# A run's last two head sums placed in front of the next run's bonus sums on TensorE

## The reference

```python
xm = xa[:, :, None] + sx[:, :, None] * (maa_stack + xxx)
xk, xw, xv, xr, xg = (xm[:, :, j] for j in range(5))
w = jnp.exp(-jnp.exp(time_decay + jnp.tanh(xw @ td_w1) @ td_w2))
r = xr @ Wr.T; k = xk @ Wk.T; v = xv @ Wv.T; g = jax.nn.silu(xg @ Wg.T)
def step(s, rkvw):
    r_t, k_t, v_t, w_t = rkvw
    a = k_t[..., :, None] * v_t[..., None, :]
    out = jnp.einsum('bhi,bhij->bhj', r_t, u * a + s)
    s = a + w_t[..., :, None] * s
    return (s, out)
```

## Time and profile before

| what | value |
|---|---|
| median of 3 runs | 1139.03 us (1138.09 to 1141.67) |
| the profiled execution | 1138.86 us, its span 1137.1 us |
| mean granted TensorE clock | 0.988 of full speed |
| busy PE, DVE, ACT, POOL | 1070.2, 910.3, 704.3, 591.4 us |
| the merged loop, bodies 0 to 15 | about 510 to 1070 us of the span |
| one body in the middle of it | 34.78 us |

### The profile page before, as it was taken

The page is one execution under the profiler, slowest core; times in us unless marked ns, Lnnn a source line. Parts: engine busy times, 40 slices in busy tenths (PEclk is TensorE's granted clock), DMA queues, the critical chain, the costliest instruction groups (busy, mean ns, idle before and its releaser), DMA issues.

```text
span 1137.1 us, 34405 instructions
## 1 busy us (share of the span) xinstructions
PE 1070.2 (94%) x12992; PEld 897.9 (79%) x12992; DVE 910.3 (80%) x1677; ACT 704.3 (62%) x1606; POOL 591.4 (52%) x520
## 2 busy tenths in 40 slices
PE   5899999999999999899999999999999998887798
PEld 4789888888889887788777778777787776666677
DVE  5987777888777784238998898988989999899964
ACT  4778787778777775455544555545565445545574
POOL 4778877877878873034444344343444443343121
PEclk9999999999999998999999999999999999889999
DMA  9400000011111110033213333123331133304011
GB/s 330 163 4 1 0 0 3 5 48 40 40 47 37 43 32 2 1 85 79 57 42 75 84 85 76 31 60 83 83 83 47 45 75 84 77 7 121 19 37 56
DMA packets 39867, 65.01 MB, mean 57 GB/s; under 512 B 4384, under 2 KB 26208, under 8 KB 39392
## 3 DMA queue, kind: packets, MB, share of 16 engines
q1 hardware_dynamic: 39776, 63.75, 21.1%
HBM read 55.35 MB, written 8.39 MB: 56 GB/s over the span
## 4 chain that ended last, share of the span: by engine, by line
PE 81%; DVE 10%; issue 5%; ACT 3%; POOL 1%; DMA 0%; DVEq 0%; ACTq 0%; POOLq 0%
PE psum L982 10%; PE psum L991 10%; PE psum L353 9%; PE psum L1071 6%; PE psum L267 5%; PE psum L336 5%; PE psum L368 5%; PE psum L297 3%; PE psum L280 3%; PE psum L1031 3%; PE psum L1109 2%; PE psum L1142 2%; PE psum L1251 2%; DVE shared L1763 2%; PE psum L310 2%
## 5 line engine op out<-in xcount | busy, mean ns | idle before, releaser
L1763 DVE TENSOR_TENSOR_SCAN shared<-late_wT,shared 128x512 f32<-128x512 f32 x128 | 169.9, 1328 | 0.0
L892 POOL TENSOR_TENSOR late_xm<-late_mixed,late_xa 128x512 f32<-128x512 f32 x64 | 91.3, 1436 | 111.4 <-DVE late_mixed L1729 111.1
L232 POOL TENSOR_TENSOR shared<-shared,att_row_max 128x512 f32<-128x512 f32 x128 | 132.6, 1056 | 17.8 <-DVE att_row_max L564 17.8
L353 PE MATMUL psum<-shared 128*128 128x128 f32 x1024 | 127.3, 278 | 1.0 <-ACT shared L462 1.0
L453 ACT ACTIVATE shared<-shared 128x512 f32<-128x512 f32 x128 | 80.5, 631 | 69.8 <-POOL shared L232 69.6
L353 PEld LDWEIGHTS psum<-shared 128*128 128x128 f32 x1024 | 121.4, 195 | 1.4 <-ACT shared L462 1.4
L982 PE MATMUL psum<-late_glnT,w 128*128 128x256 f32 x512 | 119.8, 387 | 1.8 <-ACT late_glnT L1359 1.8
L991 PE MATMUL psum<-w,late_hT 128*128 128x256 f32 x512 | 118.6, 380 | 1.0 <-ACT late_hT L1368 0.9
L564 DVE TENSOR_REDUCE att_row_max<-shared 128x8 f32<-128x512 f32 x128 | 86.8, 680 | 40.5 <-POOL shared L225 40.5
L901 POOL TENSOR_TENSOR shared<-shared,late_rT 128x512 f32<-128x512 f32 x32 | 40.7, 1273 | 142.7 <-DVE shared L1763 142.7
L982 PEld LDWEIGHTS psum<-late_glnT,w 128*128 128x128 f32 x512 | 95.9, 192 | 18.1 <-issue 2.8
(11 more groups left out here) (167 smaller groups left out, 2436.6 us busy)
## 6 DMA issues: line engine op xcount, KB each, us to landing
shared<-v_rows SPq DMA_DIRECT2D x64, 512.0 KB, 7.4
shared<-in_enc SPq DMA_DIRECT2D x64, 128.0 KB, 2.6
v_rows<-shared SPq DMA_DIRECT2D x64, 64.0 KB, 1.8
out<-x SPq DMA_DIRECT2D x16, 256.0 KB, 2.0
x<-in_x SPq DMA_DIRECT2D x7, 512.0 KB, 10.1
w<-in_w SPq DMA_DIRECT2D x2, 1024.0 KB, 16.9
shared<-in_cross_mask SPq DMA_DIRECT2D x1, 1024.0 KB, 11.6
shared<-in_w_qkv SPq DMA_DIRECT2D x1, 768.0 KB, 4.6
```

Source lines behind the costliest of these rows:

```text
L232: nc.gpsimd.tensor_tensor(zs, zs, peak.unsqueeze(2).to_broadcast([P, PAIRS, S]), ALU.subtract).then_inc(shifted, 1)
L353: last = nc.tensor.matmul(dst[:, half * P:(half + 1) * P], w[:, kb, c0 + half * P:c0 + (half + 1) * P], src[:, u % 2, kb, 0:P], start=(kb ...
L892: nc.gpsimd.tensor_tensor(xm[m % XM].rearrange("p h (b t) -> p (h b) t", t=S), mixed[:, m % 2, :, :].rearrange("p h (b t) -> p (h b) t", t=S),
L1763: nc.vector.tensor_tensor_scan(states, wT[:, u, half, :, :, :].rearrange("p j b t -> p (j b t)"), states, 0.0, ALU.mult, ALU.add).then_inc ...
```

## The change

In PE's body the two calls of `sum_heads` for run s-1 stand ahead of `bonus_sums(s)` instead of behind it. Nothing else is different, on any engine: the same instructions, the same waits, the same buffers.

```diff
                 if early(s):
                     ch_transpose(early_run(s, 0), 0)
-                if now:
-                    bonus_sums(s)
                 if old:
                     sum_heads(s - 1, 2)
                     sum_heads(s - 1, 3)
+                if now:
+                    bonus_sums(s)
                 if there(s - 2):
                     project_out(s - 2)
```

## The result

The changed kernel takes 1127.48 us in the median of 7 executions (1123.08 to 1130.46), the kernel before beside it 1139.31 (7 executions, 1136.76 to 1142.15). The ratio is 0.9894, with a 95% interval of 0.9874 to 0.9914: faster by 1.1%. The prediction was 1128.0, with a range of 1124.5 to 1132.5. The profiled execution took 1127.48 us with a span of 1125.7, 11.38 us less than the one of before.

What follows compares the result with a forecast made beforehand. PE was taken to bound the middle of the loop, VectorE bodies 13 to 15. Eleven bodies at 1.00 us give 11.0: 1138.86 - 11.0 = 1127.9, with 0.17 for the median 1128.0 us; range 1124.5 to 1132.5.

Steps and rivals of the forecast that it cites:

- The bound and the place: Bodies 2 to 12: PE bounds, its one listed wait the bonus sums for VectorE's gate, 11 times, 9.0 us.
- the 11.0 of the sum: Whole kernel: 11 bodies gain 1.00 us each, 11.0 us; body 1 and bodies 13 to 15 gain nothing.
- The hole from start to start: PE between WgT and the bonus sums: 0.97 us a body counted by group starts, against 0.81 idle in the row.
- the restart's 0.08: Bonus sums on PE: 1.04 us after the wait against 0.96 without, so 0.08 may go with the wait.
- Narrow and wide groups, net 0: PE's weight switches cost 0.08 into narrow and about 0.10 into wide; same two before and after, net 0.
- The margin of 0.11 at the bonus sums: Bonus sums could start at 713.43 and are allowed to at 713.32, so no wait for the gate is left.
- rival A: A new wait, as at the bonus sums, takes part: gain 0.3 to 0.8 a body, 1130.2 to 1135.6 us; chance 0.08.
- The margin at L1031: `mix_pair` in the middle bodies: residual L1826 reaches PE about 721.15, L1031 wants to start at 721.36; free by 0.2.
- VectorE catches up: VectorE gains 0.84 at L1729 and makes up the other 0.16 at its waits for keys and at L1697.
- Rival B: VectorE becomes the bound, deciding under 32.2 us a body; if its gaps were rigid, 1139, no change; chance 0.04.
- The last bodies, nothing: Bodies 13 to 15: PE waits for VectorE anyway, no gain or loss; L1782 covered by 0.12 in body 15.
- Rival C: TensorE's clock in bodies 13 to 15: a half-speed stretch moves, 3.2 us either way, 1124.8 to 1131.2; chance 0.07.

Runs made afterwards that it cites:

- The kernel with exchanged banks: Against the kernel before, order kept: bonus sums and output projection exchange PSUM banks, so the bonus sums need no gate; 1127.76 us, ratio 0.9924.
- the kernel with fewer switches: Changed kernel with the mixer's matmuls, narrow group first, directly behind the head sums, ahead of bonus sums and output projection; 1129.1 us, ratio 0.993.
- the two late gates: Changed kernel with VectorE's gate of run s-2 moved behind the second scan and read (1172.97 us), or only behind that scan (1145.5 us).
- the two half changes: Kernel before with the swap only in bodies 2 to 12 (1127.34 us, ratio 0.9914), or only in 1 and 13 to 15 (1138.62 us, 1.0006).
- the half cover: Kernel before with only one of the two head sums moved ahead of the bonus sums, the other left behind; 1135.9 us, ratio 0.9967.
- the kernel with the late gate: Changed kernel with VectorE's gate of run s-2 later by one key_values, one scan and one read; 1172.97 us, ratio 1.0302.

## Why the prediction was right

- *The bound and the place.* Right: PE bounds the bodies 2 to 12 and had one wait there. With the swap in these bodies alone they were as short as with the whole change, with it in the others alone nothing was gained.
- *The time.* 1128.0 against 1127.48 is closer than the parts deserve, and that is luck. The eleven bodies gave 0.57 more than the 11.0 of the sum, body 1 another 0.15 and the start of the loop 0.55, which the change can't explain; the last bodies took 0.89 back.
- *The size.* The hole from start to start, 0.97, with the restart's 0.08 makes 1.05, and 1.02 to 1.06 were measured. I had taken 1.00 of bounds of 0.82 and 1.07. The idle time in PE's row, 0.82, would have been a fifth too small. The kernel with exchanged banks shows both parts without a new order.
- *Narrow and wide groups, net 0.* Right: the old order without the wait has the same body. Their size is larger than the 0.18 that I had read for a pair. Into narrow weights it is 0.09 (1.82 against 1.73 for WgT), out of them 0.10 on the wide group (0.97 against the 0.87 that the bonus sums take behind a wide group in the kernel with fewer switches), and another 0.11 on the narrow group itself (the head sums take 1.00 in front of a wide group and 0.89 in front of a narrow one). That is 0.30, near the 0.32 of that kernel.
- *The margin of 0.11 at the bonus sums.* Measured 0.10; no wait in any body (rival A did not come about; its lower gain was 11 x 0.3 = 3.3 us and not 3.4). The margin at L1031, forecast at 0.2, was 0.13, and the kernel with fewer switches used it up. What a lost margin costs the two late gates show: 1.57 us for 1.53 us of wait.
- *VectorE catches up.* Right in the result, wrong in a number: its wait for the keys was to stay at 0.7 to 0.9 and fell to 0.34. The step was that VectorE's work from L1729 on keeps its length. The scan behind L1729 took 2.00 instead of 1.54 (at 726.43 in the trace of before), since it met GpSimd at another moment. 0.88 - 0.16 - 0.46 = 0.26 is near the 0.34. Rival B's point, 32.2 us for a body, is therefore too low: 33.73 - 0.34 - 0.78 = 32.6.
- *The last bodies, nothing.* Wrong by 0.9 of the 11.6 us. L1782 did not wait for the bonus sums, as predicted. But of the 0.71 that body 13 lost, 0.50 lies between WgT and the second part of the mixer: L1031 starts 955.81 - 941.42 = 14.39 behind WgT, where it was 13.89, and waits 4.96 us for the residual L1826 instead of 4.46. On VectorE the step is one scan, which meets GpSimd's L875 0.22 us after that began, and not 0.73 after, and takes 1.89 instead of 1.38. The sum took every duration on VectorE as fixed. That this comes from the middle bodies, and not from the swap in body 13, the two half changes show. The remaining 0.21, and the 0.18 of body 14, come behind L1031; the stretch at the half clock lies over other groups there, but that it is their cause is not shown.
- *Rival C, the clock.* In the two profiled executions it changed nothing: 0.988 of full speed in both, and 0.93 over the 46.30 us in both. The seven executions of the changed kernel have mean clocks of 0.983 to 0.992 and times of 1130.46 to 1123.08, in that order; the one in the middle had 0.988 and 1127.48. From kernel to kernel the executions spread over 1.6 to 7.4 us, and that is the noise of the comparisons here. So differences of a few us, such as 3.8 by the ratio against 4.6 by the bodies for the half cover, are told apart by the length of the bodies alone.

## What to carry to other kernels

Where the bounding engine waits for another, look in its own order for work that needs no such wait, and count the hole from start to start, not by the idle time in the row: that gives how much cover is wanted and what it brings. Look at the wait's cause too, since a shared buffer can be the whole of it, and exchanging two banks here did the same as the new order. Check how late the delayed instruction becomes for its own readers, above all in the stages that another engine bounds, and don't take that engine's durations as fixed when the work beside it moves.

## What the runs showed of the hardware

**A wait of 2.27 us, once in 37 us of otherwise full work, can take TensorE's clock to the half level.** In the kernel with the late gate eleven bodies had this wait in the same place. In the first of them the granted clock stayed at 1.00; in the ten that followed it fell to the half level and cost 1.56 us per body beyond the wait. In body 14 a wait of 2.14 at the bonus sums left the next groups at 1.00 again. A wait of 1.53 in the same place, and the 0.81 of the kernel before, left the clock at the full level in all eleven bodies. So the length of the wait does not decide alone, and what else does no run here shows. The Trainium skill, page "TensorE: Matmul & The Clock Gate", section "🎯 Why this matters for your kernels", advises against idle gaps of TensorE between bursts of matmuls, and the gap that it names is longer than 2.27 us. Here 2.27 was too much ten times out of eleven; the measurement decides.

**VectorE's scan and a GpSimd sum don't run beside each other.** Whichever began second took longer, by nearly all the time that the first still had to run: 2.00 and 2.09 against 1.22 for the scan in the middle bodies (0.92 and 1.01 us were left), 1.89 and 1.38 in body 13 (0.82 and 0.31 left), 2.11 against 1.18 and 2.20 against 1.26 for the sums (1.12 left in both). The addition is 0.14 to 0.19 us less than what was left in all six. The Trainium skill, page "SBUF — State Buffer", section "🔬 SBUF: two separate sides", states this as an exclusive lock on a port pair that both share: who starts first has it for the whole instruction, and a VectorE operation with two SBUF inputs takes part against a GpSimd operation that reads SBUF. The runs agree with it in these six cases; the port itself they can't show. Moving TensorE's work by 1 us a body was enough to change how much of the one fell on the other, which cost nothing where TensorE is the bound and 0.5 us where VectorE is.
